# Retention regrouped: score groups that fill four PSUM banks, value products of eight heads in one bank

## The chip, the cores and the metric

The kernel runs on one core of a Trainium2 chip. The metric is device time in microseconds (us) of one launch. TensorE is written PE, VectorE DVE, ScalarE ACT, GpSimd POOL, and the queue that issues the DMAs SP.

## The reference, cut to what matters

The input x has 32 sequences of 256 tokens and 128 channels. Two layers follow each other. Each computes `x = x + s * silu(f)`, where s is the attention-like branch and f the feed-forward branch of the layer normed x. Layer 0 has a softmax attention over 256 tokens and a token-shifted gate. Layer 1 has the retention that is regrouped here, and a soft mixture of 8 experts (128 slots, hidden width 512) whose result is the gate. The retention:

```
scores = einsum('bhtd,bhsd->bhts', q, k) * mask          # 16 heads, depth 8, causal with decay
denom  = clip(abs(scores).sum(-1), 1.0, 50000.0)
ret    = einsum('bhts,bhsv->bthv', scores / denom, v)    # 16 value columns a head
ret    = ret * rsqrt(mean(ret * ret, -1) + EPS)
out    = ((x @ W_g + b_g) * ret) @ W_o + b_o
```

## The kernel before, in words

**Tiling and order.** Two sequences (512 tokens) are one pair, so there are 16 pairs. A step of the program holds one visit of every task, and a step's tasks belong to different pairs: an entry `(task, index, age)` of `ORDER` works on pair `step - age`, age 0 being layer 0, age 1 most of layer 1, age 2 its end. There are 18 steps, the first and the last two of them partly empty. `ORDER` has one hand-fixed list for PE, DVE, ACT and POOL each, and each engine goes strictly through its own; nothing is reordered at run time. A task waits on semaphores for its inputs and for the last reader of what it overwrites. `BANK` says which of four PSUM banks a PE task writes, and `claim` makes it wait until the task that had that bank before it in the PE list has been read (`READ_BY`). Four more banks are one tensor, `bank_s`, for the retention's scores alone.

**Retention before.** Per pair there are 8 quads, 4 for each of the two sequences; a quad is 4 heads. POOL makes the keys of a quad with the other heads zeroed (`km_`, L323, four buffers). `quad` (L990, L993) computes its scores with PE in 32-row tiles, one head to a bank of `bank_s`: first key block against 256 queries (256 columns), second key block against the last 128 (128 columns). DVE's `ret_` (L661) multiplies the 4 x 384 numbers by the causal mask into `ret`. ACT's `ab` (L485) takes their absolute value. POOL's `add` (L329) adds the two key blocks' absolute values where they overlap. `g` (L1008) does the value products and the sums for the denominator with PE in 32-column tiles, a quad in half a bank; ACT's `RTc` (L490) copies that to `RT`. `row` turns it, and `rowd` on DVE, `urs` on POOL (power of -0.5, 128x16) and `gated` on DVE norm and gate it. `ret` and `ret_abs` have two buffers.

**The neighbours that the prediction walks through.** In layer 0: `mix` (DVE, L556, inputs in SBUF both), `local` (PE, L874), then on DVE `field` (L587), `rvg` (L606, both inputs in SBUF), `prod` (L612), `x1` (L617), `stat2` (L533, L538), then `xn2` (L627) and `xn3` (L637). In layer 1: `qk` (PE, L908) and its reader `qkc` (DVE, L644); `h` (PE, L959), `hb` (DVE, L726), `hg` (ACT, L480), `eo` (PE, L969), `eoc` (DVE, L737) for the experts; `LT`, `LTm`, `DTe`, `DT`, `mx`, `mxT` and `cs` (DVE, L717, both inputs in SBUF) for the two softmaxes; `out` (PE, L979), read by `z`. PE's transposes are at L823, L864, L942, L1018 and L1027.

Of the kernel before, what the change touches and what calls it, by code (L numbers as in the profile page):

```python
# [32 lines left out]
def columns(*widths):  # L33
    out, at = {}, 0
    for name, n in widths:
# [25 lines left out]
           ("row", 2, 1), ("gatedT", 0, 1), ("row", 3, 1), ("out", 0, 1), ("xn2T", 0, 0), ("out", 1, 1)],  # L61
    "DVE": [("z", 1, 2), ("stat", 0, 0), ("qkc", 0, 1), ("qkc", 1, 1), ("gated", 2, 2), ("vgc", 0, 1),
            ("LTm", 0, 1), ("LTm", 1, 1), ("ret", 0, 1), ("drec", 0, 1), ("attn", 0, 2), ("gated", 3, 2),
            ("vgc", 1, 1), ("xn", 0, 0), ("drec", 1, 1), ("LTm", 2, 1), ("zg", 0, 2), ("ret", 1, 1),
            ("attn", 1, 2), ("mx", 0, 1), ("LTm", 3, 1), ("drec", 2, 1), ("vgc", 2, 1), ("mx", 1, 1), ("mx", 2, 1),
            ("drec", 3, 1), ("vgc", 3, 1), ("ret", 2, 1), ("rmax", 0, 1), ("ret", 3, 1), ("cs", 0, 1),
            ("cs", 1, 1), ("mix", 0, 0), ("cs", 2, 1), ("ret", 4, 1), ("gbias", 0, 0), ("hb", 0, 1),
            ("rowd", 0, 1), ("hb", 1, 1), ("ret", 5, 1), ("hb", 2, 1), ("rowd", 1, 1), ("hb", 3, 1), ("eoc", 0, 1),
            ("sg", 0, 2), ("hb", 4, 1), ("ka", 0, 0), ("smax", 0, 0), ("eoc", 1, 1), ("smax", 1, 0),
            ("gated", 0, 1), ("ret", 6, 1), ("srowc", 0, 0), ("hb", 5, 1), ("ret", 7, 1), ("rv", 0, 0),  # L70
# [13 lines left out]
    "POOL": [("urs", 2, 2), ("urs", 3, 2), ("km", 0, 1), ("rstd", 0, 0), ("km", 1, 1), ("dn", 0, 1), ("km", 2, 1),
             ("dn", 1, 1), ("add", 0, 1), ("km", 3, 1), ("add", 1, 1), ("dn", 2, 1), ("dn", 3, 1), ("km", 4, 1),
             ("add", 2, 1), ("mixa", 0, 0), ("add", 3, 1), ("km", 5, 1), ("urs", 0, 1), ("add", 4, 1), ("km", 6, 1),
             ("add", 5, 1), ("km", 7, 1), ("urs", 1, 1), ("add", 6, 1), ("add", 7, 1), ("rstd2", 0, 0),
             ("rnorm", 0, 0)],
# [3 lines left out]
BANK = {("DT", 0): 3, ("DT", 1): 3, ("DT", 2): 0, ("DT", 3): 2, ("LT", 0): 0, ("LT", 1): 3, ("LT", 2): 1,  # L92
# [4 lines left out]
        ("local", 0): 0, ("mxT", 0): 1, ("o", 0): 2, ("o", 1): 1, ("out", 0): 0, ("out", 1): 2, ("qk", 0): 3,  # L97
        ("qk", 1): 2, ("r", 0): 2, ("rB", 0): 3, ("row", 0): 2, ("row", 1): 0, ("row", 2): 2, ("row", 3): 1,
        ("s", 0): 1, ("score", 0): 3, ("score", 1): 1, ("slots", 0): 1, ("slots", 1): 2, ("srow", 0): 0,
        ("v", 0): 2, ("vg", 0): 1, ("vg", 1): 3, ("vg", 2): 2, ("vg", 3): 0, ("xn2T", 0): 3, ("xn3T", 0): 0,  # L100
        ("xnT", 0): 0}
# [1021 lines left out]
```

## Time and profile before

| | us |
|---|---|
| median of 3 runs (lowest to highest) | 1098.94 (1097.99 to 1099.03) |
| the profiled execution's own time | 1098.24 |
| its span | 1096.4 |

| engine | busy us | share of the span | instructions |
|---|---|---|---|
| PE | 1062.8 | 97% | 10436 |
| PE weight load | 832.9 | 76% | 10436 |
| DVE | 960.2 | 88% | 2074 |
| ACT | 773.0 | 71% | 1450 |
| POOL | 606.9 | 55% | 619 |

Busy time is the time in which at least one instruction of the engine ran. The matmuls' ends are modelled and run into the next one's start, so what a task of PE costs is read from one start to the next. A line Lnnn is a line of the kernel.

### The profile page before, as it was taken

To read this page: it belongs to the slowest core of one execution; us is meant where nothing else is said; L and a number is where in the kernel's file an instruction comes from. 1 tells how busy PE (TensorE), PEld (TensorE's weight loads), DVE (VectorE), ACT (ScalarE), POOL (GpSimd) and SP (SyncE) were. 2 spreads that over 40 slices of the span, in tenths; PEclk is the share of its full clock that TensorE was granted. 3 is DMA by queue.
4 is the path that set the end of the run, shared out by engine and by line. 5 is a ranking of instruction groups with operands and counts; after the bars stand their busy time and mean duration, and the time that the engine had idled before them with its cause. 6 is when DMAs were issued, how large, how long until landed. Compare 5 with 4: busy or idle time off the path is not lost.

```text
span 1096.4 us, 27975 instructions
## 1 busy us (share of the span) xinstructions
PE 1062.8 (97%) x10436; PEld 832.9 (76%) x10436; DVE 960.2 (88%) x2074; ACT 773.0 (71%) x1450; POOL 606.9 (55%) x619
## 2 busy tenths in 40 slices
...
DMA packets 18468, 16.97 MB, mean 15 GB/s; under 512 B 800, under 2 KB 17440, under 8 KB 18080
## 3 DMA queue, kind: packets, MB, share of 16 engines
...
## 4 chain that ended last, share of the span: by engine, by line
PE 90%; DVE 6%; issue 1%; ACT 1%; POOL 0%; POOLq 0%; DVEq 0%; ACTq 0%
PE bank L1008 12%; PE bank L959 11%; PE bank L969 10%; PE bank_s L990 7%; PE bank L950 5%; PE bank L979 5%; PE bank L920 5%; PE bank L913 5%; PE bank L1035 3%; DVE ret L661 3%; PE bank L908 3%; PE bank L823 3%; PE bank L874 3%; PE bank L1018 3%; PE bank_s L993 2%; PE bank L854 2%
## 5 line engine op out<-in xcount | busy, mean ns | idle before, releaser
L329 POOL TENSOR_TENSOR ret_abs<-ret_abs 128x512 f32<-128x512 f32 x128 | 168.7, 1318 | 238.2 <-ACT ret_abs L485 238.2
L661 DVE TENSOR_TENSOR ret<-bank_s,k_sb 128x1536 f32<-128x1536 f32 x128 | 223.9, 1749 | 23.7 <-PE bank L1008 14.8
L334 POOL TENSOR_TENSOR urs<-uvar,mhalf 128x16 f32<-128x16 f32 x64 | 185.3, 2903 | 91.8 <-DVE uvar L677 91.8
L485 ACT ACTIVATE ret_abs<-ret 128x1536 f32<-128x1536 f32 x128 | 189.6, 1481 | 8.8 <-DVE ret L661 8.8
L959 PE MATMUL bank<-slotsT,w_sb 128*128 128x128 f32 x1024 | 140.9, 281 | 0.3 <-DVE hact L726 0.3
L969 PEld LDWEIGHTS bank<-w_sb,hact 128*128 128x128 f32 x1024 | 125.5, 192 | 14.7 <-issue 13.9
L969 PE MATMUL bank<-w_sb,hact 128*128 128x128 f32 x1024 | 134.1, 277 | 0.0
L959 PEld LDWEIGHTS bank<-slotsT,w_sb 128*128 128x128 f32 x1024 | 124.3, 192 | 10.3 <-issue 7.4
L340 POOL TENSOR_SCALAR dT<-dT,drec 128x256 f32<-128x256 f32 x128 | 83.4, 665 | 48.6 <-DVE drec L721 48.4
L1008 PE MATMUL bank<-ret,vrow 128*32 128x256 f32 (+1 forms) x2048 | 108.6, 329 | 0.3 <-DVE hact L726 0.2
L990 PE MATMUL bank_s<-qT,km 32*128 32x256 f32 x1024 | 91.4, 426 | 5.0 <-DVE ret L661 5.0
L726 DVE TENSOR_TENSOR hact<-bank,v_sb 128x512 f32<-128x512 f32 x128 | 87.4, 684 | 6.7 <-PE bank L959 5.3
L1008 PEld LDWEIGHTS bank<-ret,vrow 128*32 128x32 f32 x2048 | 59.7, 109 | 42.7 <-issue 5.0
L480 ACT ACTIVATE hact<-hact 128x512 f32<-128x512 f32 x128 | 79.8, 624 | 8.1 <-DVE hact L726 7.8
L446 ACT ACTIVATE cT<-bank 128x512 f32<-128x512 f32 x64 | 38.2, 597 | 58.1 <-PE bank L920 55.8
L1008 PE MATMUL bank<-ret_abs,k_sb 128*32 128x256 f32 x1024 | 79.2, 379 | 0.0
L990 PEld LDWEIGHTS bank_s<-qT,km 32*128 32x128 f32 x1024 | 40.4, 183 | 50.4 <-issue 48.2
L490 ACT ACTIVATE RT<-bank 128x256 f32<-128x256 f32 x128 | 48.0, 375 | 40.6 <-PE bank L1008 40.6
L323 POOL TENSOR_SCALAR km<-kT,k_sb 128x256 f32<-128x256 f32 x128 | 69.5, 543 | 6.9 <-DVE kT L644 6.8
L913 PE MATMUL bank<-w_sb,xn2T 128*128 128x512 f32 x128 | 66.1, 598 | 0.0
L461 ACT ACTIVATE dT<-cT,ltmax 128x256 f32<-128x256 f32 x128 | 64.0, 509 | 0.0
L979 PE MATMUL bank<-eorow,cT 128*128 128x129 f32 x512 | 62.3, 275 | 0.0
...
## 6 DMA issues: line engine op xcount, KB each, us to landing
...
w_sb<-w SPq DMA_DIRECT2D x2, 2048.0 KB, 14.8
...
```

Source lines behind the costliest of these rows:

```text
L329: pool.tensor_tensor(both[:, :, P:SEQ], both[:, :, P:SEQ], both[:, :, SEQ:3 * P], ALU.add)\
L334: pool.tensor_tensor(urs[:, j], uvar[:, j], mhalf[:], ALU.pow).then_inc(ready["urs"].sem, 1)
L340: ins = pool.tensor_scalar(dT[:, m % 2, b], dT[:, m % 2, b], drec[:, m, b:b + 1], 1.0, ALU.mult, ALU.mult)
L485: act.activation(ret_abs[:, q % MR], ret[:, q % MR], ACT.Abs).then_inc(ready["ab"].sem, 1)
L661: dve.tensor_tensor(ret[:, q % MR], bank_s[:, :, 0:3 * P], causal.unsqueeze(1).broadcast_to([P, Q, 3 * P]), ALU.mult)\
L726: dve.tensor_tensor(hact[:, e % 2], bank[:].rearrange("p (c n) -> p c n", c=HC), V["b1"][:, e * HC:(e + 1) * HC].unsqueeze(2).broadcast_to ...
L913: pe.matmul(bank[:], xn2T[:, j // 2, (j % 2) * P:(j % 2 + 1) * P], W["vg"], start=True, stop=True)\
L959: ins = pe.matmul(bank[:, c * P:(c + 1) * P], w1_sb[:, e, c * P:(c + 1) * P], slotsT[:, e // 2, 2 * (e % 2):2 * (e % 2) + 2].rearrange("p ...
L969: ins = pe.matmul(bank[:, i * C:(i + 1) * C], hact[:, i, c], w2_sb[:, e, c], start=(c == 0), stop=(c == HC - 1))
L979: ins = pe.matmul(bank[:, i * (C + 1):(i + 1) * (C + 1)], cT[:, m, j * P:(j + 1) * P], eorow[:, m, b], start=(m == 0), stop=(m == E // 2 - 1))
L990: pe.matmul(bank_s[:, n, 0:SEQ], km[rows, q % KM, 0:P], qT[par][rows, b], start=True, stop=True)
L1008: ins = pe.matmul(bank[n * HT:(n + 1) * HT, sblock * P:SEQ], left, src[:, q % MR, n, cols[0]:cols[1]], start=(phase == 0), stop=(phase == 2))
```

## The change

Quads are no longer the unit. For each sequence there are three score groups, and each fills all of `bank_s`: group 0 is the second key block of all 16 heads (16 products of 128 columns), groups 1 and 2 are the first key block of 8 heads each (8 products of 256 columns). DVE and ACT read 2048 columns at a time instead of 1536, 6 times a pair instead of 8. The results are in `low` and `high` with their absolute values in `low_abs` and `high_abs`, each with one buffer where `ret` had two. POOL's addition comes 4 times a pair with 8 x 128 numbers instead of 8 times with 4 x 128. The value products of 8 heads share one bank, so there are 4 of these tasks instead of 8, and 4 copies to `RT` of 512 columns instead of 8 of 256. `z` and `zt` no longer have their own memory but lie in the two buffers of `hact`, with a wait for it in `hb`. All four `ORDER` lists and `BANK` are new. The matmuls themselves, their number and their columns, are the same.

```diff
-            def quad(p, par, q):
-                b = q // Q
+            def scores(p, par, a):
+                b, i = divmod(a, 3)
+                quads = range(Q * b, Q * b + Q) if i == 0 else range(Q * b + 2 * i - 2, Q * b + 2 * i)
                 pe.wait_ge(*ready["qkc"](p, 0))
-                pe.wait_ge(*ready["km"](p, q))
-                since(pe, ready["ret"], *((p, q - 1) if q else (p - 1, QUADS - 1)))
...
+                pe.wait_ge(*ready["km"](p, quads[-1]))
+                since(pe, ready["ret"], *((p, a - 1) if a else (p - 1, GROUPS - 1)))
+                for u, q in enumerate(quads):
+                    for n in range(Q):
+                        rows = slice(n * HT, (n + 1) * HT)
+                        if i == 0:
+                            ins = pe.matmul(bank_s[:, n, u * P:(u + 1) * P], km[rows, q % KM, P:SEQ], qT[par][rows, b, P:SEQ],
+                                            start=True, stop=True)
+                        else:
+                            ins = pe.matmul(bank_s[:, n, u * SEQ:(u + 1) * SEQ], km[rows, q % KM, 0:P], qT[par][rows, b],
+                                            start=True, stop=True)
+                ins.then_inc(filled["A"].sem, 1)
...
+            def values(p, par, h):
+                b, half = divmod(h, 2)
+                pe.wait_ge(*ready["add"](p, h))
+                pe.wait_ge(*ready["vgc"](p, 2 * b + 1))
+                bank = claim("gg", p, h)
+                for u in range(2):
+                    i = 2 * half + u
+                    for phase in range(3):
+                        for n in range(Q):
+                            left = vrow[:, 2 * b + phase, Q * i + n] if phase < 2 else K["count"]
+                            right = (high[:, n, u], low[:, n, i], high_abs[:, n, u])[phase]
...
-            def add(p, par, q):
-                pool.wait_ge(*ready["ab"](p, q))
...
+            def add(p, par, h):
+                b, half = divmod(h, 2)
+                pool.wait_ge(*ready["ab"](p, 3 * b))
+                pool.wait_ge(*ready["ab"](p, 3 * b + 1 + half))
+                pool.tensor_tensor(high_abs[:, :, :, P:SEQ], high_abs[:, :, :, P:SEQ], low_abs[:, :, 2 * half:2 * half + 2], ALU.add)\
                     .then_inc(ready["add"].sem, 1)
...
+            def ret_(p, par, a):
+                b, i = divmod(a, 3)
+                dve.wait_ge(*filled["A"](p, a))
+                flat = bank_s[:].rearrange("p n m -> p (n m)")
+                if i == 0:
+                    since(dve, filled["gg"], *((p, 1) if b else (p - 1, 3)))
...
+                else:
+                    h = 2 * b + i - 1
+                    since(dve, filled["gg"], *((p, h - 1) if h else (p - 1, HALVES - 1)))
...
+                if e < 2:
+                    since(dve, ready[("zg", "sg")[e]], p - 1)
```

The new lists in the stretches that the prediction walks through (A is a score group, gg a value product of 8 heads):

```diff
+    "PE": [("gg", 3, 2), ("eo", 6, 2), ("row", 2, 2), ("xn2T", 0, 1), ("eo", 7, 2), ("row", 3, 2), ("qk", 0, 1),
+           ("qk", 1, 1), ("xn3T", 0, 1), ("out", 0, 2), ("out", 1, 2), ("vg", 0, 1), ("LT", 0, 1), ("xnT", 0, 0),
+           ("A", 0, 1), ("LT", 1, 1), ("s", 0, 0), ("vg", 1, 1), ("A", 1, 1), ("LT", 2, 1), ("o", 0, 2),
+           ("vg", 2, 1), ("DT", 0, 1), ("LT", 3, 1), ("A", 2, 1), ("e", 0, 0), ("DT", 1, 1), ("r", 0, 0),
+           ("gatedT", 1, 2), ("gg", 0, 1), ("DT", 2, 1), ("DT", 3, 1), ("global", 0, 0), ("mxT", 0, 1),
...
+           ("k", 0, 0), ("row", 0, 1), ("score", 0, 0), ("h", 1, 1), ("A", 4, 1), ("eo", 0, 1),
+           ("h", 2, 1), ("score", 1, 0), ("eo", 1, 1), ("h", 3, 1), ("A", 5, 1), ("row", 1, 1), ("srow", 0, 0),
+           ("PT", 0, 0), ("gg", 2, 1), ("PT", 1, 0), ("v", 0, 0), ("eo", 2, 1), ("local", 0, 0), ("h", 4, 1),
+           ("eo", 3, 1), ("h", 5, 1), ("h", 6, 1), ("gatedT", 0, 1), ("eo", 4, 1), ("h", 7, 1), ("eo", 5, 1)],
+    "DVE": [("hb", 7, 2), ("xn2", 0, 1), ("stat", 0, 0), ("xn3", 0, 1), ("rowd", 2, 2), ("eoc", 3, 2),
+            ("qkc", 0, 1), ("qkc", 1, 1), ("rowd", 3, 2), ("z", 0, 2), ("xn", 0, 0), ("gated", 2, 2), ("z", 1, 2),
...
+            ("ret", 1, 1), ("drec", 1, 1), ("attn", 0, 2), ("LTm", 2, 1), ("mix", 0, 0), ("vgc", 2, 1),
+            ("drec", 2, 1), ("gated", 3, 2), ("LTm", 3, 1), ("mx", 0, 1), ("drec", 3, 1), ("zg", 0, 2),
...
+            ("rowd", 0, 1), ("hb", 1, 1), ("ret", 4, 1), ("hb", 2, 1), ("smax", 0, 0), ("smax", 1, 0),
+            ("eoc", 0, 1), ("hb", 3, 1), ("cs", 2, 1), ("srowc", 0, 0), ("ka", 0, 0), ("rowd", 1, 1),
+            ("gated", 0, 1), ("ret", 5, 1), ("rv", 0, 0), ("srec", 0, 0), ("gated", 1, 1), ("cs", 3, 1),
+            ("field", 0, 0), ("rvg", 0, 0), ("hb", 4, 1), ("eoc", 1, 1), ("prod", 0, 0), ("hb", 5, 1),
+            ("x1", 0, 0), ("stat2", 0, 0), ("hb", 6, 1), ("eoc", 2, 1)],
...
+        ("o", 1): 0, ("out", 0): 2, ("out", 1): 0, ("qk", 0): 2, ("qk", 1): 3, ("r", 0): 0, ("rB", 0): 0,
```

Of the tasks with bank 2, `qk 0` is the one just ahead of `out 0` in the new PE list, so `out 0` waits for `qkc 0`. On ACT the list has `ab 1` after `LTc 2`, `DTe 3`, `Dc 1`, `gTc 1`, `tr` in this order, and `PTc 1`, `ab 5`, `tv`, `sp`. On POOL it has `dn 1`, `add 0`, `dn 2`, and ends with `urs 1`, `add 3`. The number of activation-table switches in ACT's list is the same, 4 a step.

## Rows read from the trace of the kernel before

**Rows 1.** Windows, one step: length, busy time (instructions) of each engine, PE clock.
```profile
499.46:565.40 65.94, 65.67 (x655) 51.75 (x653) 59.75 (x129) 48.06 (x90) 37.75 (x39) 1.00 0.03 10
```

**Rows 2.** Waits of PE: us in total, times, longest.
```profile
PE bank_s L990 <- DVE ret L661: 5.0, 16, 0.6
```

**Rows 3.** Timeline of PE around one quad: start, duration, engine, line, instructions.
```profile
503.77 0.59 PE L920 MATMUL bank<-xn3T,slot_sb 128*128 128x256 f32 x2
504.30 0.71 PE L990 MATMUL bank_s<-qT,km 32*128 32x256 f32 x8
504.83 0.40 PE L993 MATMUL bank_s<-qT,km 32*128 32x128 f32 x8
505.16 1.16 PE L1035 MATMUL bank<-w_sb,gatedT 128*128 128x128 f32 x8
506.16 0.60 PE L920 MATMUL bank<-xn3T,snT 128*128 128x256 f32 x2
```

**Rows 4.** Timeline of PE around value products and experts.
```profile
543.78 0.86 PE L1008 MATMUL bank<-ret,vrow 128*32 128x256 f32 x16
...
546.08 1.16 PE L959 MATMUL bank<-slotsT,w_sb 128*128 128x128 f32 x8
547.07 0.60 PE L864 MATMUL bank<-k_sb,prob 128*128 128x128 f32 x4
...
552.08 1.95 PE L874 MATMUL bank<-srow,probT 128*128 128x128 f32 x16
553.87 1.06 PE L969 MATMUL bank<-w_sb,hact 128*128 128x128 f32 x8
554.76 1.06 PE L959 MATMUL bank<-slotsT,w_sb 128*128 128x128 f32 x8
555.75 0.86 PE L1008 MATMUL bank<-ret,vrow 128*32 128x256 f32 x16
```

**Rows 5.** Groups by line: busy us, mean ns of one, idle before.
```profile
L329 POOL TENSOR_TENSOR ret_abs<-ret_abs 128x512 f32<-128x512 f32 x128 | 168.7, 1318 | 238.2 <-ACT ret_abs L485 238.2
L661 DVE TENSOR_TENSOR ret<-bank_s,k_sb 128x1536 f32<-128x1536 f32 x128 | 223.9, 1749 | 23.7 <-PE bank L1008 14.8
L485 ACT ACTIVATE ret_abs<-ret 128x1536 f32<-128x1536 f32 x128 | 189.6, 1481 | 8.8 <-DVE ret L661 8.8
L726 DVE TENSOR_TENSOR hact<-bank,v_sb 128x512 f32<-128x512 f32 x128 | 87.4, 684 | 6.7 <-PE bank L959 5.3
```

**Rows 6.** Timeline of DVE after `local`.
```profile
554.07 1.12 DVE L587 SCALAR_TENSOR_TENSOR spin<-bank,srec,srow 128x128 f32<-128x128 f32 x4 [0.17 <-PE bank L874]
555.11 1.04 DVE L606 SCALAR_TENSOR_TENSOR prob<-prob 128x512 f32<-128x512 f32 x1
556.08 0.68 DVE L726 TENSOR_TENSOR hact<-bank,v_sb 128x512 f32<-128x512 f32 x1
556.68 0.67 DVE L612 SCALAR_TENSOR_TENSOR spin<-spin,prob 128x512 f32<-128x512 f32 x1
...
559.43 1.72 DVE L737 TENSOR_TENSOR eorow<-bank,v_sb 64x256 f32<-64x256 f32 x4
...
564.18 0.17 DVE L670 TENSOR_SCALAR den<-bank 128x16 f32<-128x16 f32 x1
...
566.28 0.86 DVE L533 BATCH_NORM_STATS2 stat<-x_sb 128x6 f32<-128x128 f32 x4
...
567.59 0.72 DVE L644 SCALAR_TENSOR_TENSOR qT<-bank,v_sb,k_sb 128x512 f32<-128x512 f32 x1
```

**Rows 7.** Timeline of POOL in the same stretch.
```profile
554.33 1.27 POOL L329 TENSOR_TENSOR ret_abs<-ret_abs 128x512 f32<-128x512 f32 x1 [2.66 <-ACT ret_abs L485]
```

**Rows 8.** Timelines of DVE and POOL at `mix`.
```profile
591.45 2.63 DVE L556 SCALAR_TENSOR_TENSOR mix<-xnT,v_sb,mix 128x512 f32<-128x512 f32 x2 [1.18 <-POOL mix L297]
...
591.38 1.26 POOL L329 TENSOR_TENSOR ret_abs<-ret_abs 128x512 f32<-128x512 f32 x1
```

**Rows 9.** Line L556: shortest, median and longest of one.
```profile
L556 DVE SCALAR_TENSOR_TENSOR mix<-xnT,v_sb,mix x32: 744/961/1752, 11.2 to 989.0; 128x512 f32<-128x512 f32 x32
```

More of the change, by code:

```diff
@@ L50 @@
 ORDER = {
[10 rows of a table removed]
[L61 to L70, printed above, removed]
[3 rows of a table removed]
@@ L84 @@
[L84 to L88, printed above, removed]
-}
-BANK = {("DT", 0): 3, ("DT", 1): 3, ("DT", 2): 0, ("DT", 3): 2, ("LT", 0): 0, ("LT", 1): 3, ("LT", 2): 1,
[4 rows of a table removed]
[L97 to L101, printed above, removed]
[10 rows of a table added]
@@ new lines @@
+    "ACT": [("RTc", 3, 2), ("hg", 7, 2), ("usq", 2, 2), ("xn2Tc", 0, 1), ("ce", 3, 2), ("usq", 3, 2),
+            ("xn3Tc", 0, 1), ("LTc", 0, 1), ("xnTc", 0, 0), ("zt", 0, 2), ("DTe", 0, 1), ("LTc", 1, 1),
+            ("sT", 0, 0), ("ab", 0, 1), ("DTe", 1, 1), ("LTc", 2, 1), ("ab", 1, 1), ("DTe", 2, 1), ("LTc", 3, 1),
+            ("eTc", 0, 0), ("Dc", 0, 1), ("DTe", 3, 1), ("Dc", 1, 1), ("gTc", 1, 2), ("tr", 0, 0), ("RTc", 0, 1),
+            ("Dc", 2, 1), ("Dc", 3, 1), ("ab", 2, 1), ("slc", 0, 1), ("slc", 1, 1), ("rBc", 0, 1), ("sgT", 0, 0),
[4 rows of a table added]
@@ new lines @@
+    "POOL": [("rstd2", 0, 1), ("rnorm", 0, 1), ("rstd", 0, 0), ("urs", 2, 2), ("km", 0, 1), ("km", 1, 1),
+             ("km", 2, 1), ("km", 3, 1), ("urs", 3, 2), ("dn", 0, 1), ("mixa", 0, 0), ("km", 4, 1), ("km", 5, 1),
+             ("dn", 1, 1), ("add", 0, 1), ("dn", 2, 1), ("dn", 3, 1), ("km", 6, 1), ("add", 1, 1), ("km", 7, 1),
+             ("urs", 0, 1), ("add", 2, 1), ("urs", 1, 1), ("add", 3, 1)],
+}
+BANK = {("DT", 0): 1, ("DT", 1): 3, ("DT", 2): 0, ("DT", 3): 2, ("LT", 0): 2, ("LT", 1): 2, ("LT", 2): 0,
[5 rows of a table added]
+        ("row", 0): 3, ("row", 1): 1, ("row", 2): 3, ("row", 3): 1, ("s", 0): 0, ("score", 0): 2,
+        ("score", 1): 0, ("slots", 0): 2, ("slots", 1): 1, ("srow", 0): 3, ("v", 0): 2, ("vg", 0): 1,
+        ("vg", 1): 1, ("vg", 2): 3, ("vg", 3): 3, ("xn2T", 0): 2, ("xn3T", 0): 0, ("xnT", 0): 3}
@@ L102 @@
 READ_BY = {"xnT": ("xnTc", 0), "s": ("sT", 0), "global": ("gbias", 0), "e": ("eTc", 0), "srow": ("srowc", 0),
            "score": "P", "PT": "PTc", "local": ("field", 0), "r": ("tr", 0), "k": ("kr", 0), "v": ("rv", 0),
-           "xn2T": ("xn2Tc", 0), "xn3T": ("xn3Tc", 0), "qk": "qkc", "vg": "vgc", "LT": "LTc", "mxT": ("rmax", 0), "rB": ("rBc", 0), "DT": "Dc", "slots": "slc", "h": "hb", "eo": "eoc", "row": "ug", "g": "RTc", "gatedT": "gTc", "o": "attn",
+           "xn2T": ("xn2Tc", 0), "xn3T": ("xn3Tc", 0), "qk": "qkc", "vg": "vgc", "LT": "LTc", "mxT": ("rmax", 0), "rB": ("rBc", 0), "DT": "Dc", "slots": "slc", "h": "hb", "eo": "eoc", "row": "ug", "gg": "RTc", "gatedT": "gTc", "o": "attn",
@@ L195, in build @@
         eorow = sb("eorow", E // 2, 2, C + 1)
-        z, zt = sb("z", TILES, C), sb("zt", TILES, C)
+        z, zt = (hact[:, i].rearrange("p c n -> p (c n)").rearrange("p (j c) -> p j c", j=TILES) for i in range(2))
         banks = [ctx.enter_context(nc.psum_tensor(f"bank{i}", [P, 512], F32)) for i in range(4)]
@@ L214, in build @@
             ("prod", 1), ("x1", 1), ("stat2", 1), ("mv2", 1), ("var_eps2", 1), ("rstd2", 1), ("rn", 3), ("rnorm", 1),
-            ("xn2", 1), ("xn3", 1), ("xn2Tc", 1), ("xn3Tc", 1), ("qkc", 2), ("km", QUADS), ("vgc", 4), ("ret", QUADS),
-            ("ab", QUADS), ("add", QUADS), ("RTc", QUADS), ("usq", 4), ("ug", 4), ("den", 4), ("den2", 4), ("ums", 4),
+            ("xn2", 1), ("xn3", 1), ("xn2Tc", 1), ("xn3Tc", 1), ("qkc", 2), ("km", QUADS), ("vgc", 4), ("ret", GROUPS),
+            ("ab", GROUPS), ("add", HALVES), ("RTc", HALVES), ("usq", 4), ("ug", 4), ("den", 4), ("den2", 4), ("ums", 4),
             ("uvar", 4), ("urs", 4), ("gated", 4), ("gTc", 2), ("attn", 2), ("LTc", 4), ("mx", 3), ("rmax", 1), ("rBc", 1), ("cs", 4), ("ce", 4),
```

95 lines of the change are left out of this document (41 added, 54 removed), and 30 rows, old and new, of tables (BANK, ORDER).

## The prediction
> **What bounds the kernel now.** I read a window of one step first. Between two starts of the first `qk` lie 65.94 us, of which PE is busy 65.67, at full clock; DVE is busy 59.75, ACT 48.06, POOL 37.75 [rows 1]. So PE sets the pace, and DVE has only 6 us to spare, which matters once DVE is late at one place. Then PE's waits: in the steady steps the only one is the score group's for DVE's `ret`, 5.0 us in 16 times, 0.3 a step [rows 2]. Then PE's timeline, read from start to start. Eight passes of 128 columns take 0.89 (553.87 to 554.76), which is 0.11 each; that is streaming [rows 4]. Since PE streams nearly always, a change gains only what it takes from PE's overheads and waits, and loses whatever it makes PE wait.
>
> **PE's own work.** The products and their columns stay, so I count overheads. Ahead of a quad the last L920 pair takes 0.53 for 4 x 0.11 = 0.44: 0.10 for the change from full array to 32-row tiles [rows 3]. The quad's starts are 0.53 + 0.33 = 0.86 apart for 6 x 0.11 = 0.66 of columns: 0.20 (its first weights are not loaded ahead, and the way out) [rows 3]. The eight passes after it take 1.00 for 0.89: 0.11 [rows 3]. Value products cost 0.10 on the way in (554.76 to 555.75 is 0.99) and 0.10 behind (546.08 to 547.07 is 0.99); a block of two, which is what `gg` is, takes 2.30 in both kernels [rows 4]. Transposes behind a block I take at half, 0.05.
> Both kernels go into a tile shape 9 times a step from the full array (before, three of the 8 quads and 4 value blocks run straight into one another; after, one of the 6 score groups and 4 value blocks does). What differs: two blocks of 32-row tiles fewer, -0.60; two more value blocks that are entered from the full array, +0.20; behind the nine blocks six matmul tasks and three transposes instead of five and four, +0.05. That is 0.35 a step less. With the old wait for `ret` gone too, which I take at 0.34 in a steady step (0.3 by the row [rows 2]), PE's step without waits is 65.94 - 0.69 = 65.25.
>
> **The readers.** `ret` takes 1.749 for 1536 columns; `hb` takes 0.684 for 512 [rows 5], so 0.53 per 512 more and 2.28 for 2048. DVE: 6 x 2.28 = 13.7 for 8 x 1.75 = 14.0. ACT's 1.481 becomes at most 4/3 of it, 1.97; I take 1.91: 11.5 for 11.8. The four wider copies to `RT` save a few tenths of ACT. POOL's addition takes 1.27 in an undisturbed case [rows 7] (mean 1.318 [rows 5]), so 2.5 for twice the numbers, half as often. None of these sums bounds the step, so they are worth nothing by themselves; what counts is that each link of the chain score group, `ret`, `ab`, `add`, `gg` is longer. It was 1.75 + 1.48 + 1.27 = 4.5 and is 2.28 + 1.91 + 2.5 = 6.7, plus handovers. The shared memory of `z` and `hact` adds waits in `hb 0` and `hb 1` for jobs that end 3 us or more before; the DMAs are the same, and the load of x has 4 us between `x1` and the next `stat`. I take both at nothing.
>
> **A walk at the end of the step.** I laid PE's new list out from the end of `gg 2` to `out 0`. Eleven tasks of eight passes (eo 2 to 7, v, h 4 to 7) at 0.89 are 9.8; `local` 1.79 (552.08 to 553.87); six transposes at 0.44 are 2.64; two `qk` with as many columns as eight passes 1.75; `gg 3` 2.30 with 0.20 around it; 0.05 behind `gg 2`. Sum 18.5 us [rows 4].
> `out 0` writes bank 2 behind `qk 0`, so it waits for DVE's `qkc 0`, and it is DVE's list that decides when that is: rvg, hb 4, eoc 1, prod, hb 5, x1, stat2, hb 6, eoc 2, hb 7, xn2, stat, xn3, rowd 2, eoc 3, qkc 0. Before, hb 7 to xn3 (one hb, prod, x1, stat2, two eoc, xn2, rowd 2, xn3) took 564.18 - 556.08 = 8.10. To this I add three hb at 0.60 (556.08 to 556.68), one eoc at 0.87 (1.72 for four halves), `stat` 1.31 (566.28 to 567.59) and qkc 0.72 [rows 6]: 12.8 from the start of hb 4 to the end of qkc 0.
> When does `rvg` end? If nothing holds it: `local` ends 4.05 after `gg 2`, `field` starts 0.20 later and takes 1.04, and `rvg` would take 0.60 (the pitch of its like), so hb 4 starts at 5.9, and qkc 0 ends at 18.7: 0.2 to 0.3 of wait with the handover of 0.1.
> But `rvg` is held. In the trace it takes 1.04 where an operation of this size takes 0.67 to 0.68 [rows 5, 6]. It starts at 555.11, POOL's addition runs from 554.33 to 555.60, and `rvg` ends at 556.15, 0.55 after that [rows 6, 7]. `mix` at 591.45 starts beside an addition that ends at 592.64; its two operations take 2.63, against 0.744 for the shortest one [rows 8, 9]. So a DVE operation with both inputs in SBUF stands still until a POOL addition that began first is done. In the new kernel `ret 5` must wait for `gg 2`: 0.2 + 2.28 + 1.94 + 2.54 puts `add 3` from 4.4 to 6.95 after the end of `gg 2`. `rvg` wants to start at 5.3, falls into it, and ends at 7.5. hb 4 starts at 7.4, qkc 0 ends at 20.2, PE goes on at 20.3 instead of 18.5: 1.8 us of wait.
> The same rule hits `cs 2`: `add 2` starts 4.3 after the end of group 4, `cs 2` comes at 6.0 and stands until 7.4 instead of 6.7. Srowc, ka, rowd 1 and gated 0 follow, and `ret 5` starts 0.3 late. So the end of the step costs 2.1. Bounds: 0.2 (nothing is held) to 2.6.
> The Trainium skill bears on this, GPSIMD Engine Reference, section 1 Specifications: GpSimd's way to SBUF is shared with VectorE, and they contend when a VectorE instruction has two SBUF inputs. Read as two engines that share at half speed each, it would let `rvg` end at 6.65, and the wait would be 0.9 shorter; the trace, with an `rvg` that ends 0.55 behind the addition, speaks for the full stop.
>
> **A walk in the middle.** `ret 1` ends 2.4 after group 1 leaves PE, and `add 0` starts 2.0 after that. DVE gets `mix` in before it, but then `gated 3` (both inputs in SBUF) stands for the rest of the addition, some 1.5 us. PE's `gatedT 1` is due 7.5 after group 1 and comes 0.3 late. LTm 3, DTe 3, Dc 1, gTc 1 and `tr` follow one another on DVE and ACT, and `DT 2`, which takes the bank that `tr` reads, is 0.3 late. Together 0.6; bounds 0 and 1.3. At other places (`gg 2` for `add 2`, `srow` for hb 3, `row 0` for `RTc 1`, group 1 for `ret 0`) I find 0 to 0.25 us to spare and take 0 for all, with 0.3 as the bound.
>
> **Sum.** 65.25 + 2.1 + 0.6 = 67.95 a step, 2.0 more than before, over 15 steps +30. Filling and draining hold the same tasks in much the same order; I take them at 0 +- 2. From the profiled execution's 1098.2 this gives 1128 us. The median of the runs is 0.7 above the profiled one, within what I can resolve. The likeliest case's own range is 65.25 + 1.3 to 65.25 + 3.6, so 1107 to 1142.
>
> **Rivals.**
> First, nothing new waits: DVE and ACT meet PE's list as well as before, and only the saved overheads and the old wait show. For it: the same kind of list kept PE at 65.67 of 65.94 [rows 1]; DVE's sum falls a little. Against it: the two walks. It gives 1098.2 - 16 x 0.69 = 1087. This is the other sign; its place are the changes of tile shape at the score groups, and it decides if the waits at `out 0` and `DT 2` together stay under 0.69 us a step. Chance 0.15.
> Second, DVE's list is late by its length alone, and POOL's additions hold it little, because they start later than I put them or are taken in turns. Then the end costs 0.3 to 1.2, the middle nothing or 0.3. It gives 65.25 + 0.9 = 66.1, or 1101, between 1096 and 1108. For it: the walk's start of `add 3` hangs on four durations, one of which (ACT on 2048 columns) is estimated. Chance 0.2.
> Third, more places are held: the additions of 2.5 us catch `mix`, `mx`, `ka` or `x2` as well. `mix` costs PE up to 1.3 if `add 0` comes 0.4 earlier. It gives over 1142. Chance 0.1.
> My forecast has 0.55.
>
> **Range and chances.** The low end takes in the second rival and the upper part of the first, the high end is that of the forecast: 1093 to 1142. Under 0.2% (2.2 us) a change can't be told from none here. Faster by more: the first rival and the lower edge of the second, 0.18. Within: 0.07. Slower: 0.75.
>
> **What would show it.** In the profile after: a step (first `qk` to first `qk`) of 67.9 with PE busy about 65.2; a wait of PE at L979 or just ahead of it for DVE of about 2 us a step, part of which may show at `h 7`, `eo 4` or `xn2T`, which hang on the same DVE list; `rvg` with 2.0 us instead of 1.04, ending 0.55 after the last addition of the step; `gated 3` with over 1 us; `ret` at 2.28, the absolute value at 1.91, the addition at 2.5; no wait of a score group for `ret`; 0.3 of overhead at each of six score groups. The prediction is wrong if `rvg` stays near 1.0 or if PE's wait in that stretch is under 0.7 a step; the first would end the rule about the held operation, the second the walk.

## The result, and the profile after

The changed kernel takes 1129.38 us (median of 4 runs, 1128.83 to 1129.93), the kernel before 1098.99 beside it (1097.99 to 1099.63): a ratio of 1.0277, 95% interval 1.026 to 1.0295. The forecast was 1128.

The profiled execution has a span of 1128.1 us. One steady step of it, as a window from one first `qk` to the next (length, busy time of PE, PEld, DVE, ACT, POOL, then clock and DMA), stands against [rows 1]:
```profile
440.26:508.18 67.92, 66.44 (x654) 51.10 (x653) 59.59 (x127) 47.94 (x85) 35.31 (x35) 1.00 0.03 9
```
The step is 67.92 instead of 65.94, so 1.98 longer. Between the second of these starts and the last lie 14 such steps; they take 27.9 of the 31.7 us by which the span grew. Up to the second start the new kernel is 3.1 us faster (100.68 against 103.74), behind the last one it is 6.8 us slower. DVE and ACT are busy a little less than before, POOL 2.4 us less, and the clock is the same: the loss isn't work, it is waiting. (PE's busy time rose by 0.77 with the same matmuls. It can't be used as a measure of PE's work here; more on that below.)

PE's waits, which answer to [rows 2] (us in total, times, longest):
```profile
PE bank L963 <- POOL dT L343: 6.0, 16, 0.7
PE bank L980 <- DVE hact L747: 5.2, 16, 0.4
PE bank L963 <- ACT rt L422: 4.0, 14, 0.3
PE bank L1052 <- DVE hact L747: 3.7, 15, 0.3
...
PE bank_s L1017 <- DVE low L675: 1.0, 2, 0.7
```
Before, the score groups' wait for `ret` was the only steady one. Now one is seen 2 times in the whole run. Four others come once in nearly every step: `DT 3` for `dn 3` on POOL, `h 7` for `hb 5`, `DT 2` for `tr`, and `gatedT 0` (L1052) for `hb 4`. (`dn`, L343, is POOL's scaling of what `DT` turns; `tr`, L422, is ACT's function of what `r` left in its bank; `drec` on DVE makes the factor for `dn`.)

The readers and the addition, by line (busy us, mean ns of one, idle before), against [rows 5]:
```profile
L332 POOL TENSOR_TENSOR high_abs<-high_abs,low_abs 128x1024 f32<-128x1024 f32 x64 | 153.3, 2395 | 131.6 <-ACT high_abs L494 131.6
L680 DVE TENSOR_TENSOR high<-bank_s,k_sb 128x2048 f32<-128x2048 f32 x64 | 146.3, 2286 | 9.0 <-PE bank_s L1017 8.3
...
L494 ACT ACTIVATE high_abs<-high 128x2048 f32<-128x2048 f32 x64 | 122.1, 1908 | 13.1 <-DVE high L680 13.0
```

Now the two places where DVE is held. First the end of the step: DVE, then POOL (start, duration, line), against [rows 6, 7]:
```profile
622.67 1.41 DVE L736 TENSOR_TENSOR cT<-cT,rB 128x512 f32<-128x512 f32 x1
...
626.57 2.28 DVE L680 TENSOR_TENSOR high<-bank_s,k_sb 128x2048 f32<-128x2048 f32 x1
...
630.82 1.13 DVE L598 SCALAR_TENSOR_TENSOR spin<-bank,srec,srow 128x128 f32<-128x128 f32 x4 [0.34 <-PE bank L895]
631.87 2.00 DVE L617 SCALAR_TENSOR_TENSOR prob<-prob 128x512 f32<-128x512 f32 x1
633.79 0.68 DVE L747 TENSOR_TENSOR hact<-bank,v_sb 128x512 f32<-128x512 f32 x1
```
```profile
621.17 2.36 POOL L332 TENSOR_TENSOR high_abs<-high_abs,low_abs 128x1024 f32<-128x1024 f32 x1 [2.33 <-ACT high_abs L494]
...
630.95 2.37 POOL L332 TENSOR_TENSOR high_abs<-high_abs,low_abs 128x1024 f32<-128x1024 f32 x1 [1.53 <-ACT high_abs L494]
```
Read the ends, not the lengths. The last addition ends at 630.95 + 2.37 = 633.32, and `rvg` (L617) at 631.87 + 2.00 = 633.87: 0.55 later. `cs 2` (L736) ends at 624.08, the addition before at 623.53: again 0.55. So each does nearly all of its work after POOL is done, and everything behind it in DVE's list is late by what it was held.

Then the middle of the step, where `gated 3` (L702) runs into `add 0`, DVE and POOL:
```profile
595.04 1.84 DVE L702 TENSOR_TENSOR gated<-ug,urs 128x256 f32<-128x256 f32 x1
...
598.72 0.67 DVE L773 SCALAR_TENSOR_TENSOR hact<-hact 128x512 f32<-128x512 f32 x1
599.31 1.48 DVE L724 TENSOR_TENSOR mx<-mx,cT 128x512 f32<-128x512 f32 x2
```
```profile
594.07 2.53 POOL L332 TENSOR_TENSOR high_abs<-high_abs,low_abs 128x1024 f32<-128x1024 f32 x1 [0.89 <-ACT high_abs L494]
...
599.00 2.13 POOL L343 TENSOR_SCALAR dT<-dT,drec 128x256 f32<-128x256 f32 x2 [1.32 <-DVE drec L740]
```
`gated 3` has half the numbers of `rvg` and ends 0.28 after the addition (596.88 against 596.60). The two instructions of `dn 3` at 599.00 show the other direction: the first begins while `zg` (L773, inputs in SBUF both) runs, and the two take 2.13, where a free one takes 0.48. `mx 1`, the first of the two at 599.31, begins after it and still goes ahead of it.

What it does to PE, in its timeline, at the end of the step and in the middle (the time in brackets is PE's idle time and its releaser):
```profile
600.20 0.63 PE L963 MATMUL bank<-k_sb,dT 128*128 128x128 f32 x4 [0.28 <-ACT rt L422]
601.19 0.66 PE L963 MATMUL bank<-k_sb,dT 128*128 128x128 f32 x4 [0.36 <-POOL dT L343]
...
634.61 0.63 PE L1052 MATMUL bank<-k_sb,gated 128*128 128x128 f32 x4 [0.25 <-DVE hact L747]
635.38 1.13 PE L990 MATMUL bank<-w_sb,hact 128*128 128x128 f32 x8
636.83 1.13 PE L980 MATMUL bank<-slotsT,w_sb 128*128 128x128 f32 x8 [0.32 <-DVE hact L747]
```
And PE's own overhead, around one score group:
```profile
584.05 0.60 PE L844 MATMUL bank<-k_sb,xn 128*128 128x128 f32 x4
584.58 1.17 PE L1014 MATMUL bank_s<-qT,km 32*128 32x128 f32 x32
585.68 0.70 PE L941 MATMUL bank<-xn3T,snT 128*128 128x256 f32 x2
```
From start to start the group takes 1.10, for which 0.88 are columns (8 times the 0.11 of [rows 4]), and the transposes ahead of it 0.53 for 0.44. So about the same 0.3 around six groups as around eight quads before [rows 3].

### The profile page after: what moved, and what is told of

Its sections match the earlier page's. It is cut to its first block, busy times and chain, and to the rows that moved or that the text cites. A ratio compares the mean times of both kernels' runs of the same rounds, so it can differ in the third digit from the quotient of the medians.

```text
span 1128.1 us, 27626 instructions
## 1 busy us (share of the span) xinstructions
PE 1073.1 (95%) x10436; PEld 821.7 (73%) x10436; DVE 959.5 (85%) x2042; ACT 770.8 (68%) x1354; POOL 574.2 (51%) x555
## 4 chain that ended last, share of the span: by engine, by line
PE 70%; DVE 17%; issue 9%; POOL 2%; ACT 1%; ACTq 0%; POOLq 0%; DVEq 0%
PE bank L1033 9%; PE bank L990 8%; PE bank L980 7%; PE bank L1000 5%; PE bank L971 5%; PE bank_s L1017 4%; PE bank L934 4%; PE bank_s L1014 3%; DVE high L680 3%; PE bank L895 3%; PE bank L941 3%; PE bank L844 3%; PE bank L1043 2%; PE bank L875 2%; PE bank L929 2%
## 5 line engine op out<-in xcount | busy, mean ns | idle before, releaser
L332 POOL TENSOR_TENSOR high_abs<-high_abs,low_abs 128x1024 f32<-128x1024 f32 x64 | 153.3, 2395 | 131.6 <-ACT high_abs L494 131.6
L680 DVE TENSOR_TENSOR high<-bank_s,k_sb 128x2048 f32<-128x2048 f32 x64 | 146.3, 2286 | 9.0 <-PE bank_s L1017 8.3
L747 DVE TENSOR_TENSOR hact<-bank,v_sb 128x512 f32<-128x512 f32 x128 | 87.7, 685 | 73.0 <-PE bank L980 69.9
L980 PE MATMUL bank<-slotsT,w_sb 128*128 128x128 f32 x1024 | 133.8, 276 | 5.2 <-DVE hact L747 5.2
L494 ACT ACTIVATE high_abs<-high 128x2048 f32<-128x2048 f32 x64 | 122.1, 1908 | 13.1 <-DVE high L680 13.0
L343 POOL TENSOR_SCALAR dT<-dT,drec 128x256 f32<-128x256 f32 x128 | 82.9, 660 | 91.7 <-DVE drec L740 91.7
L675 DVE TENSOR_TENSOR low<-bank_s,k_sb 128x2048 f32<-128x2048 f32 x32 | 73.3, 2292 | 10.0 <-PE bank L1033 6.2
L1033 PE MATMUL bank<-high,vrow 128*32 128x256 f32 x1024 | 80.2, 385 | 1.4 <-POOL high_abs L332 1.4
L1033 PE MATMUL bank<-high_abs,k_sb 128*32 128x256 f32 x1024 | 78.7, 379 | 0.0
L1017 PE MATMUL bank_s<-qT,km 32*128 32x256 f32 x1024 | 73.3, 400 | 1.0 <-DVE low L675 1.0
L500 ACT ACTIVATE RT<-bank 128x512 f32<-128x512 f32 x64 | 38.0, 594 | 39.2 <-PE bank L1033 39.2
L490 ACT ACTIVATE low_abs<-low 128x2048 f32<-128x2048 f32 x32 | 61.1, 1910 | 2.2 <-DVE low L675 1.3
```

The source lines that it names most:

```text
L332: pool.tensor_tensor(high_abs[:, :, :, P:SEQ], high_abs[:, :, :, P:SEQ], low_abs[:, :, 2 * half:2 * half + 2], ALU.add)\
L343: ins = pool.tensor_scalar(dT[:, m % 2, b], dT[:, m % 2, b], drec[:, m, b:b + 1], 1.0, ALU.mult, ALU.mult)
L494: ins = act.activation(high_abs[:], high[:], ACT.Abs)
L680: ins = dve.tensor_tensor(high[:].rearrange("p n i m -> p (n i) m"), flat.rearrange("p (u m) -> p u m", m=SEQ), causal[:, 0:SEQ].unsqueeze ...
L747: dve.tensor_tensor(hact[:, e % 2], bank[:].rearrange("p (c n) -> p c n", c=HC), V["b1"][:, e * HC:(e + 1) * HC].unsqueeze(2).broadcast_to ...
L980: ins = pe.matmul(bank[:, c * P:(c + 1) * P], w1_sb[:, e, c * P:(c + 1) * P], slotsT[:, e // 2, 2 * (e % 2):2 * (e % 2) + 2].rearrange("p ...
```

## The experiments

My theory: the step is longer because three DVE operations whose two inputs both lie in SBUF (`gated 3`, `cs 2`, `rvg`) stand still until an addition of POOL that began first has ended, and the additions are now twice as long. The rival: DVE's list is late by its length and the longer chain from score group to value products, and the held operations only hide slack. Every time stands beside runs of the kernel before on the same chip; ratios are to it, with the 95% interval. All kernels are the changed one with an edit, except the last. "Step" is the distance of two first `qk` in the steady part, the median of the 14; what I call a wait below is the surplus in the distance of two starts on PE's timeline over that of the same two tasks when nothing is late.

**One: `rvg` behind two operations that read PSUM.**
```diff
-            ("field", 0, 0), ("rvg", 0, 0), ("hb", 4, 1), ("eoc", 1, 1), ("prod", 0, 0), ("hb", 5, 1),
+            ("field", 0, 0), ("hb", 4, 1), ("eoc", 1, 1), ("rvg", 0, 0), ("prod", 0, 0), ("hb", 5, 1),
```


> The changed kernel with one entry of DVE's list moved: rvg comes behind hb 4 and eoc 1 instead of ahead of them. Theory (a DVE operation with two SBUF inputs stands still until a POOL addition that began first is done): rvg then starts when add 3 is over, takes 0.68 instead of 2.00 us, and the waits of PE at gatedT 0, eo 4 and h 7 (1.3 us a step) go. Step 67.92 -> 66.6, time 1129 -> 1109 to 1111. Rival (DVE's list is only too long; the order within it is worth nothing): the chain to qkc 0 keeps its length, step 67.7 or more, time 1125 to 1129.


Measured: 1114.07 us (1113.82 to 1114.86), 1.0145 (1.013 to 1.016); step 66.87. DVE and POOL at that place:
```profile
623.18 0.68 DVE L747 TENSOR_TENSOR hact<-bank,v_sb 128x512 f32<-128x512 f32 x1
623.93 0.86 DVE L758 TENSOR_TENSOR eorow<-bank,v_sb 64x256 f32<-64x256 f32 x2
624.82 0.69 DVE L617 SCALAR_TENSOR_TENSOR prob<-prob 128x512 f32<-128x512 f32 x1
```
```profile
622.26 2.38 POOL L332 TENSOR_TENSOR high_abs<-high_abs,low_abs 128x1024 f32<-128x1024 f32 x1 [1.52 <-ACT high_abs L494]
```
`hb 4` (L747) and `eoc 1` (L758), with one input in PSUM, run beside the addition at their full speed, and `rvg`, which starts when the addition is over (624.64), takes 0.69. One moved entry gives 15 us back, half of the loss; the same DVE work in the same amount is on the list, so length alone can't be the cause. The time is 3 us above what I expected: `h 7` still waits 0.26 for `hb 5`, with 0.07 behind it, and `xn3T` and `out 0` wait 0.23 together.

**Two: `gated 3` ahead of `ret 1`.**
```diff
-            ("ret", 1, 1), ("drec", 1, 1), ("attn", 0, 2), ("LTm", 2, 1), ("mix", 0, 0), ("vgc", 2, 1),
-            ("drec", 2, 1), ("gated", 3, 2), ("LTm", 3, 1), ("mx", 0, 1), ("drec", 3, 1), ("zg", 0, 2),
+            ("gated", 3, 2), ("ret", 1, 1), ("drec", 1, 1), ("attn", 0, 2), ("LTm", 2, 1), ("mix", 0, 0), ("vgc", 2, 1),
+            ("drec", 2, 1), ("LTm", 3, 1), ("mx", 0, 1), ("drec", 3, 1), ("zg", 0, 2),
```


> The changed kernel with gated 3 moved ahead of ret 1 in DVE's list, where DVE is idle 0.3 us and POOL adds nothing. Theory: gated 3 takes 0.42 instead of 1.84 us, LTm 3, DTe 3, dn 3 and tr come over 0.5 us earlier, and PE's waits at DT 2 and DT 3 (0.85 us a step) mostly go. Step 67.92 -> 67.1 to 67.3, time 1116 to 1120. mx 0 will now fall into the addition and takes part of it back. Rival (the sum of DVE's work decides): 1128 to 1130.


Measured: 1120.64 us (1119.87 to 1121.04), 1.0201 (1.0184 to 1.0218); step 67.25. No `gated` is held any more (shortest, median and longest of one, ns):
```profile
L702 DVE TENSOR_TENSOR gated<-ug,urs x64: 408/416/426, 82.1 to 1111.2; 128x256 f32<-128x256 f32 x64
```
`DT 2` no longer waits for `tr`, and of the wait of `DT 3` for `dn 3` 0.20 of 0.50 stays: 8.7 us back, 0.6 us less than the least that I had expected.

**Three: `cs 2` behind `cs 1`.**
```diff
-            ("sg", 0, 2), ("hb", 0, 1), ("vgc", 3, 1), ("x2", 0, 2), ("cs", 0, 1), ("cs", 1, 1), ("ret", 3, 1),
+            ("sg", 0, 2), ("hb", 0, 1), ("vgc", 3, 1), ("x2", 0, 2), ("cs", 0, 1), ("cs", 1, 1), ("cs", 2, 1), ("ret", 3, 1),
...
-            ("eoc", 0, 1), ("hb", 3, 1), ("cs", 2, 1), ("srowc", 0, 0), ("ka", 0, 0), ("rowd", 1, 1),
+            ("eoc", 0, 1), ("hb", 3, 1), ("srowc", 0, 0), ("ka", 0, 0), ("rowd", 1, 1),
```


> The changed kernel with cs 2 alone moved, from behind hb 3 (where it meets add 2) to behind cs 1. Theory: cs 2 takes 0.68 instead of 1.41 us; srowc, ka, rowd 1, gated 0, ret 5, ab 5 and add 3 come earlier by up to 0.2 us (ret 5 has to wait for gg 2 anyway), and PE's wait ahead of local (0.35 us a step) goes. Step 67.95 -> 67.5 to 67.7, time 1122 to 1126. Rival (cs 2 lies in slack, as ret 5 waits for gg 2): 1128 to 1130.


Measured: 1126.48 us (1125.99 to 1126.77), 1.0255 (1.0241 to 1.0269); step 67.76. `cs` takes 0.68, and the wait ahead of `local` (0.29, with 0.07 behind it) is gone, yet only 2.9 us came back. DVE, then POOL:
```profile
629.90 2.19 DVE L617 SCALAR_TENSOR_TENSOR prob<-prob 128x512 f32<-128x512 f32 x1
```
```profile
629.18 2.37 POOL L332 TENSOR_TENSOR high_abs<-high_abs,low_abs 128x1024 f32<-128x1024 f32 x1 [1.79 <-ACT high_abs L494]
```
`local` comes earlier, so `rvg` comes earlier, falls deeper into the same addition (0.72 after its start instead of 0.92), and is held 0.2 longer. A gain ahead of a held operation is eaten by the hold. That is why the three moves can't be judged one by one.

**Four: all three moves together.** No further edit.


> The changed kernel with three entries of DVE's list moved out of POOL's additions: rvg behind eoc 1, gated 3 ahead of ret 1, cs 2 behind cs 1. Same instructions in all. Theory: the three holds (2.00 - 0.68, 1.84 - 0.42, 1.41 - 0.68) go and with them PE's waits but for 0.2 to 0.5 us a step: step 65.5 to 65.8, time 1092 to 1098, at or below the kernel before (1099). Rival (too little slack on DVE since the regrouping, whatever the order): over 1115.


Measured: 1098.14 us (1097.71 to 1098.59), 0.9997 (0.9987 to 1.0006). The window of one step:
```profile
560.15:626.01 65.86, 65.73 (x654) 50.97 (x653) 56.80 (x128) 47.63 (x85) 36.13 (x35) 1.00 0.03 10
```
DVE's busy time falls from 59.59 to 56.80 with the same instructions on its list. By the single operations, the three that were held are shorter by 1.31, 1.43 and 0.73, and `mx 0` is longer by 0.31, because `add 0` now holds it (1.13 instead of 0.82). Three entries moved in DVE's list take away the whole loss of 30 us; the time is that of the kernel before, at the upper edge of what I expected. Left are `DT 3` 0.20 for `dn 3`, `h 7` 0.26 for `hb 5` with 0.07 behind it, and the 0.23 at `xn3T` and `out 0`.

**Five: the addition in two instructions of half the size,** with the lists as changed.
```diff
-                pool.tensor_tensor(high_abs[:, :, :, P:SEQ], high_abs[:, :, :, P:SEQ], low_abs[:, :, 2 * half:2 * half + 2], ALU.add)\
-                    .then_inc(ready["add"].sem, 1)
+                for u in range(2):
+                    ins = pool.tensor_tensor(high_abs[:, :, u, P:SEQ], high_abs[:, :, u, P:SEQ], low_abs[:, :, 2 * half + u], ALU.add)
+                ins.then_inc(ready["add"].sem, 1)
```


> The changed kernel with POOL's addition given as two instructions of 512 numbers instead of one of 1024; lists as they are. Theory (DVE waits for the end of the POOL instruction that began first): rvg gets in between the halves, 0.75 us instead of 2.00; gated 3 takes 0.5 to 0.6 instead of 1.84; cs 2 falls into the second half and stays near 1.4. POOL's second halves start later. Step 67.92 -> 66.0 to 66.3, time 1100 to 1105. Rival (the two engines share the way to SBUF at some rate, so only the total overlap counts): the total of the additions is the same or 0.1 longer, time 1127 to 1131.


Measured: 1107.19 us (1106.37 to 1108.99), 1.0083 (1.0068 to 1.0098); step 66.39. DVE, then POOL (`rvg` is L618 here):
```profile
620.37 0.90 DVE L618 SCALAR_TENSOR_TENSOR prob<-prob 128x512 f32<-128x512 f32 x1
```
```profile
619.45 2.96 POOL L333 TENSOR_TENSOR high_abs<-high_abs,low_abs 128x512 f32<-128x512 f32 x2 [1.52 <-ACT high_abs L495]
```
POOL's work and the chain to the value products are as long as before or longer, and still nearly three quarters of the loss (22.2 us) go: `rvg` waits for the first half only, gets in between the two, and now the second half waits for it (2.96 for the two instead of 2.50 at 609.53). The unit of the hold is one instruction. The time is 2.2 us above the most that I had expected; `cs 2` falls into the second half, takes 1.55, and `local` comes 0.43 late for it (the way there is told below).

**Six: an addition with one input.** The second key block's absolute values are left out of the denominator; POOL multiplies the same 1024 numbers by 1 instead.
```diff
-                pool.tensor_tensor(high_abs[:, :, :, P:SEQ], high_abs[:, :, :, P:SEQ], low_abs[:, :, 2 * half:2 * half + 2], ALU.add)\
+                pool.tensor_scalar(high_abs[:, :, :, P:SEQ], high_abs[:, :, :, P:SEQ], 1.0, 1.0, ALU.mult, ALU.mult)\
```


> The changed kernel, lists as they are; POOL's addition is replaced by a multiplication of the same 1024 numbers by 1, so that it reads one SBUF input. The part left out is the second key block in the denominator. Theory A (DVE's operation with two SBUF inputs is held only by a POOL operation that has two as well): rvg falls to 0.7 to 0.8 us, gated 3 to 0.45, cs 2 to 0.8, step 65.8 to 66.1, time 1097 to 1101. Theory B (any POOL operation holds it until its end): POOL's operation takes about 1.8 us instead of 2.4, the holds shrink by 0.6 each, time 1110 to 1118.


Measured: 1095.22 us (1094.68 to 1095.55), 0.9971 (0.996 to 0.9982); step 65.79. DVE, then POOL:
```profile
613.14 0.89 DVE L617 SCALAR_TENSOR_TENSOR prob<-prob 128x512 f32<-128x512 f32 x1
```
```profile
602.82 1.05 POOL L332 TENSOR_SCALAR high_abs<-high_abs 128x1024 f32<-128x1024 f32 x1 [2.35 <-ACT high_abs L494]
```
The time lies under both of my ranges. The operation took 1.05 us, not the 1.8 that I had expected, so the time tests less than it was meant to: `rvg` overlaps POOL for 0.35 only. But the 15 overlapping cases are clear on one point. They end 0.54 after POOL's operation and take 0.881 to 0.893, for overlaps of 0.345 to 0.357. Held to its end, that is 0.54 + 0.35 = 0.89; two engines at half speed would give 0.68 + 0.18 = 0.86. So a POOL operation with one input holds DVE in the same way; what frees this kernel is that it is short. `mx` and `dn` in the changed kernel say the same: with a `dn` (one input) in progress for another 0.16, 0.28 or 0.40, `mx` takes 0.70, 0.82 or 0.94, which is 0.54 and the whole of the overlap each time; at half speed it would be 0.76, 0.82 and 0.88.

**Seven: the three moves and the halves.**


> The kernel with the three moves of DVE's list and in addition POOL's addition in two instructions of 512 numbers. Theory: of what is still held only mx 0 (1.13 us) is in the middle of an addition; it falls to about 0.9, the waits of PE that are left are of other kinds (h 7 for hb 5, DT 3 for dn 3, xn3T for eoc 3). Time within 2 us of the three moves alone, 1096 to 1099. If the holds were more than the three found, it would gain over 3 us.


Measured: 1099.64 us (1099.16 to 1100.48), 1.0012 (1.0003 to 1.0021); step 65.88. The time is 0.6 us above my range and 1.5 above that of experiment four. `mx 0`, which I had expected to fall to 0.9, takes 1.28, as it now falls into the first half. The shorter instructions bring nothing once the three operations are out of the way, so the halves had helped against those holds and nothing else.

**Eight: the three moves, and what was still late.** `hb 5` goes ahead of `rvg` as well (for `h 7`), and `stat` behind `qkc 1`, with POOL's `rstd` behind `km 0` (for `xn3T` and `out 0`).
```diff
-    "DVE": [("hb", 7, 2), ("xn2", 0, 1), ("stat", 0, 0), ("xn3", 0, 1), ("rowd", 2, 2), ("eoc", 3, 2),
-            ("qkc", 0, 1), ("qkc", 1, 1), ("rowd", 3, 2), ("z", 0, 2), ("xn", 0, 0), ("gated", 2, 2), ("z", 1, 2),
+    "DVE": [("hb", 7, 2), ("xn2", 0, 1), ("xn3", 0, 1), ("rowd", 2, 2), ("eoc", 3, 2),
+            ("qkc", 0, 1), ("qkc", 1, 1), ("stat", 0, 0), ("rowd", 3, 2), ("z", 0, 2), ("xn", 0, 0), ("gated", 2, 2), ("z", 1, 2),
...
-            ("field", 0, 0), ("rvg", 0, 0), ("hb", 4, 1), ("eoc", 1, 1), ("prod", 0, 0), ("hb", 5, 1),
+            ("field", 0, 0), ("hb", 4, 1), ("eoc", 1, 1), ("hb", 5, 1), ("rvg", 0, 0), ("prod", 0, 0),
...
-    "POOL": [("rstd2", 0, 1), ("rnorm", 0, 1), ("rstd", 0, 0), ("urs", 2, 2), ("km", 0, 1), ("km", 1, 1),
+    "POOL": [("rstd2", 0, 1), ("rnorm", 0, 1), ("urs", 2, 2), ("km", 0, 1), ("rstd", 0, 0), ("km", 1, 1),
```


> The kernel with the three moves, and two more against the waits of PE that are left (0.76 us a step): hb 5 goes ahead of rvg and prod (h 7 waits for it, 0.26), and stat 0 goes from ahead of xn3 to behind qkc 1, with rstd 0 behind urs 2 and km 0 on POOL (xn3T and out 0 wait for eoc 3 and qkc 0, 0.23). Theory (PE's own work is 65.13 us a step and every wait removed shows in full): step 65.89 -> 65.4, time 1098 -> 1090 to 1092. Rival (the moves only shift a wait to the next bank or to km 3 ahead of the first score group): 1096 to 1100.


Measured: 1094.35 us (1092.3 to 1095.05), 0.9957 (0.9943 to 0.997). The window of a step, and in the filling a wait of PE that wasn't there:
```profile
560.30:625.59 65.29, 65.25 (x654) 50.86 (x653) 56.87 (x128) 47.74 (x85) 36.11 (x34) 1.00 0.03 10
```
```profile
44.91 0.66 PE L844 MATMUL bank<-k_sb,xn 128*128 128x128 f32 x4 [3.00 <-DVE xn L560]
```
This version beats both kernels, by 4.1 us against the one before. The step came out as expected, the whole over 2 us higher than I expected: from the first `qk` to the second it is 67.2 us, where it is 63.0 in experiment four, since `stat` comes later in DVE's list. The 14 steps behind that bring 8.4, and the first takes 4.2 of it back.

**Nine: the same rule on the kernel before.** There `mx 1` is held by `add 1`; `vgc 3` goes ahead of it.
```diff
-            ("attn", 1, 2), ("mx", 0, 1), ("LTm", 3, 1), ("drec", 2, 1), ("vgc", 2, 1), ("mx", 1, 1), ("mx", 2, 1),
-            ("drec", 3, 1), ("vgc", 3, 1), ("ret", 2, 1), ("rmax", 0, 1), ("ret", 3, 1), ("cs", 0, 1),
+            ("attn", 1, 2), ("mx", 0, 1), ("LTm", 3, 1), ("drec", 2, 1), ("vgc", 2, 1), ("vgc", 3, 1), ("mx", 1, 1), ("mx", 2, 1),
+            ("drec", 3, 1), ("ret", 2, 1), ("rmax", 0, 1), ("ret", 3, 1), ("cs", 0, 1),
```


> The kernel before with one entry of DVE's list moved: vgc 3 goes ahead of mx 1, which so starts 0.67 us later and meets only the end of POOL's add 1. Theory: the one wait of the kernel before (a quad for ret 2, 0.34 us a step) was itself such a hold: mx 1 took 1.55 instead of 0.7 us. mx 1 now takes about 0.9, ret 2 comes 0.65 earlier, the wait goes, step 65.95 -> 65.6, time 1098.5 -> 1093 to 1094. Rival (that wait comes from DVE's load ahead of ret 2 and not from the hold): 1098 to 1099.


Measured: 1096.98 us (1096.03 to 1097.82), 0.9984 (0.9975 to 0.9993). The hold is short now (`mx 1` takes 0.90 instead of 1.55, the two `mx` 1.78 instead of 2.44), and quad 3's wait for `ret` is gone, but a new wait of PE has its place, and the step stays at 65.96:
```profile
PE bank L959 <- DVE gbias L563: 3.2, 15, 0.2
```
The mechanism was as expected, the gain was not: the next hold eats it. Counted from the first `qk`, `ret 2` starts 0.66 earlier and `ret 3` 0.35. But the addition that `cs 0` meets begins where it did, so the pair `cs 0`, `cs 1` takes 1.96 instead of 1.61, and `mix` and `gbias` come no earlier. PE gets to `h 1` 0.36 earlier, whose bank `gbias` has yet to read, and waits that long. The 1.8 us that the kernel gains don't lie in the step.

## Why the prediction was right, and where it was not

**PE's own work: right, a little small.** A step without its waits is 67.92 - 2.82 = 65.10 by the surpluses below, against 65.94 - 0.34 = 65.60 before. The regrouping saves 0.5 and I had 0.35; where the other 0.15 comes from I haven't followed. The old wait is gone as forecast. Experiment eight shows the saving as time: 65.30 with 0.20 of waits.

**The durations: right.** `ret` 2.286 (forecast 2.28), the absolute value 1.908 (1.91), the addition 2.395 (2.5), `rvg` 2.00 (2.0), `cs 2` 1.41 (held from 6.7 to 7.4, which is the same 0.7).

**The end of the step: the sum right, the places not.** Forecast 2.1, measured 1.96. I had put it at `out 0`. It falls where PE first meets the late list: `local` 0.36 for `PTc 1`, `gatedT 0` 0.41 for `hb 4`, `eo 4` 0.33 for `eoc 1`, `h 7` 0.63 for `hb 5` (with 0.07 behind it), and only 0.23 is left for `xn3T` and `out 0`. `gatedT 0`, `eo 4` and `h 7` together are 1.37 late, about as much as `rvg` is held (1.32). Experiment one takes 1.05 of it away; the rest is `h 7`, for which `hb 5` comes late without a hold too. The term for `cs 2` was right in size (0.3) and wrong in its way, as ACT and PE show (start, duration):
```profile
624.11 0.63 ACT L458 ACTIVATE cT<-cT 128x512 f32<-128x512 f32 x1 [0.48 <-DVE cT L736]
...
628.07 0.59 ACT L412 ACTIVATE probT<-bank 128x512 f32<-128x512 f32 x1
...
628.76 2.02 PE L895 MATMUL bank<-srow,probT 128*128 128x128 f32 x16
```
It isn't a late `ret 5`. `ce 2` (L458) waits for the held `cs 2`, and behind it in ACT's list stand `hg 2`, `RTc 2`, `hg 3` and `PTc 1` (L412), for which `local` (L895) waits: it starts 0.10 after `PTc 1` ends. In experiment three, with `cs 2` free, it starts 0.24 after it and waits for nothing.

**The middle: too small.** Forecast 0.6, measured 0.86. `gated 3` was held as I said (1.84), but `gatedT 1` isn't late, since it is due just after. The failed step is that I followed only the chain to `tr`: `DT 2` is late by 0.36 for it, as forecast, but `DT 3` by 0.50 for `dn 3`. `LTm 3`, `DTe 3` and `drec 3` come late, and then `dn 3` is itself held by DVE's `zg` and `mx 1`. I had used the rule in one direction only. In all, 1.96 + 0.86 = 2.82 where 2.7 were forecast.

**The total: nearer than its terms.** The forecast step of 67.95 meets 67.92 because errors cancel: PE's work 0.15 too high, the end 0.14 too high, the middle 0.26 too low. The same holds for the whole: 15 steps of 2.0 and nothing for the rest were forecast, and 27.9 in 14 steps and 3.8 for the rest came. That the total is right to 2 us is partly luck; the two terms for held operations are not.

**PE's busy time: wrong as a sign.** I wanted 65.2 of busy time in a step of 67.9; the row shows 66.44. Short waits lie partly inside modelled matmuls, so busy time and idle time can't be split at this scale, and starts have to be compared. The Trainium skill warns against matmul busy time as a measure of how near a kernel is to its roofline, as matmuls are pipelined (Perfetto Trace Analysis, Identifying the Most-Contended Engine). It is no measure here either: 1062.8 before and 1073.1 after for the same matmuls.

**The rivals.** The first (1087, nothing new waits) fell with the two walks; but its 1087 is what the saving on PE would give, and experiment eight got a part of it. The second (additions taken in turns, or starting late) is refuted by the rows and by experiments one, four and five. The third (`mix` and `mx` held too) did not come: `mix` starts ahead of `add 0`, and it and `mx 0` only meet a `dn`, which holds them for 0.10 and 0.14. `mx 0` is held by the addition once `gated 3` is moved (experiment four).

**The shared memory of `z` and `hact`** showed no wait in the trace. A kernel with memory of its own for them wasn't tried. That it costs nothing is therefore argued, not shown. What the 3.8 us outside the 14 steps are made of stays open too.
